# Taking all filler products off TensorE in a four-layer latent-attention kernel

## The reference, cut to what matters

```python
x = x + _L0_xattn_ref(_layernorm(x), ctx_1024, ctx_1024, fside, mask, ...)   # weighted, masked attention
x = x + _L0_attn_ref(_layernorm(x), ...)      # second-order Taylor attention
x = x + _L0_ffn_ref(_layernorm(x), ...)       # router and 8 experts, top 2
x = x + _L1_xattn_ref(_layernorm(x), ...)     # masked attention
x = x + _L1_attn_ref(_layernorm(x), ...)      # 16 heads of 64, block-causal
x = x + _L1_ffn_ref(_layernorm(x), ...)       # experts choose their tokens
x = x + _L2_xattn_ref(...)                    # key-masked attention
x = x + _L2_attn_ref(_layernorm(x), ...)      # plain attention
x = x + _L2_ffn_ref(_layernorm(x), ...)       # zone-weighted experts
x = x + _L3_xattn_ref(_layernorm(x), ...)
x = x + _L3_attn_ref(_layernorm(x), ...)      # gated recurrence over tokens
x = x + _L3_ffn_ref(_layernorm(x), ...)       # two-layer MLP
```

## Time and profile before

| | before |
|---|---|
| median of three executions | 1602.1 us (1601.02 to 1603.36) |
| the profiled execution, its own time | 1599.94 us |
| its span, first to last instruction | 1598.0 us |
| mean granted TensorE clock | 0.963 |
| PE busy | 1451.5 us (91%) |
| VectorE, ScalarE, GpSimd busy | 992.6, 713.4, 384.8 us |

### The profile page before, as it was taken

How to read it: one execution, slowest core, us unless ns; L and a number is a source line. 1 busy time by engine, 2 the same in 40 slices (tenths; PEclk the granted TensorE clock), 3 DMA queues, 4 the chain that set the end, 5 groups by cost and what they waited for, 6 DMA issues and landing times. The chain is left out here.

```text
span 1598.0 us, 29795 instructions
## 1 busy us (share of the span) xinstructions
PE 1451.5 (91%) x11197; PEld 845.2 (53%) x11296; DVE 992.6 (62%) x2290; ACT 713.4 (45%) x964; POOL 384.8 (24%) x548
## 2 busy tenths in 40 slices
PE   8899997999999988599999888499999896999987
PEld 3665653555555555255555464235555582555555
DVE  4544446888888744677777233298886235888842
ACT  4144130444444431166565442146767221667662
POOL 4543141666666620100000021111100001011000
PEclk9999997999999997799999999789999997999999
DMA  8888993434336043254552196146667611566700
GB/s 263 250 268 247 274 302 117 61 61 61 61 61 153 2 73 47 50 83 74 84 85 36 35 283 211 50 68 100 90 100 212 100 19 43 80 98 92 142 19 7
DMA packets 130377, 178.22 MB, mean 112 GB/s; under 512 B 14109, under 2 KB 105269, under 8 KB 123062
## 3 DMA queue, kind: packets, MB, share of 16 engines
q1 hardware_dynamic: 117802, 161.10, 47.7%
q10 hardware_dynamic: 12432, 15.21, 2.9%
HBM read 132.44 MB, written 43.78 MB: 110 GB/s over the span
## 5 line engine op out<-in xcount | busy, mean ns | idle before, releaser
L808 ACT ACTIVATE prob_a<-ps 128x1024 f32<-128x1024 f32 x512 | 505.2, 1023 | 304.3 <-PE ps L693 193.0
L676 PE MATMUL ps<-kop,qop 116*128 116x512 bf16 x1024 | 341.9, 404 | 57.1 <-PEq L529 33.3
L821 DVE CUSTOM_DVE_ANT_0 dump_a<-ps,neg_q 128x512 bf16<-128x512 f32 (+1 forms) x485 | 328.7, 717 | 98.5 <-PE ps L676 97.0
L690 PE MATMUL ps<-qop,kop 116*128 116x256 bf16 x2048 | 349.3, 274 | 10.2 <-ACT prob_a L808 4.9
L825 DVE TENSOR_REDUCE best_a<-ps 128x1 f32<-128x512 f32 (+1 forms) x488 | 312.6, 709 | 59.0 <-PE ps L676 58.9
L690 PEld LDWEIGHTS ps<-qop,kop 116*128 116x128 bf16 x2048 | 195.2, 100 | 137.3 <-ACT prob_a L808 18.0
L676 PEld LDWEIGHTS ps<-kop,qop 116*128 116x128 bf16 x1024 | 86.9, 100 | 216.8 <-issue 95.8
L715 PE MATMUL ps<-prob_a,vop_a 128*32 128x256 f32 x3072 | 185.0, 382 | 0.0
L920 POOL TENSOR_TENSOR used_a<-prob_a,gT 128x1024 f32<-128x1024 f32 x64 | 151.3, 2364 | 87.5 <-DVE used_a L838 67.4
L693 PE MATMUL ps<-neg_k,identb 128*128 128x512 bf16 x425 | 161.8, 381 | 0.0
L899 POOL CAST mpart_a<-nmax_a 128x2 bf16<-128x2 f32 x64 | 25.3, 396 | 560.1 <-DVE nmax_a L830 560.1
(11 more groups left out here) (309 smaller groups left out, 1296.4 us busy)
## 6 DMA issues: line engine op xcount, KB each, us to landing
kop<-kparts SPq DMA_DIRECT2D x448, 128.0 KB, 5.2
kparts<-kp SPq DMA_DIRECT2D x64, 384.0 KB, 4.5
vals<-vst SPq DMA_DIRECT2D x16, 1024.0 KB, 7.0
vraw<-vals SPq DMA_DIRECT2D x64, 256.0 KB, 6.4
e_w<-in_e_w SPq DMA_DIRECT2D x6, 2048.0 KB, 16.1
z_w<-in_z_w SPq DMA_DIRECT2D x24, 256.0 KB, 7.2
ctxT<-in_ctxT SPq DMA_DIRECT2D x8, 512.0 KB, 8.0
raw<-in_mask ACTq DMA_DIRECT2D x8, 512.0 KB, 5.9
```

The lines of the kernel that those rows point to most:

```text
L676: return pe.matmul(out, qop[0:R_ALL, h, t * P:(t + 1) * P], kop[0:R_ALL, h % UNROLL, j * CHUNK:(j + 1) * CHUNK], start=True, stop=True)
L690: ins = pe.matmul(st_bank(n)[:, j * NT:(j + 1) * NT], kop[0:R_ALL, h % UNROLL, k * P:(k + 1) * P], qop[0:R_ALL, h, :], start=(j % 2 == 0), ...
L808: act.activation(prob[:, n % NP, :], st_bank(n), ACT.Exp).then_inc(S("exp_done"), 1)
L821: dve.tensor_tensor_reduce(out=dump[:, k % 2, 0:width], in0=bank, in1=c.neg_q[:, t, j * CHUNK:j * CHUNK + width], scale=1.0, scalar=-3.0e3 ...
```

## The change

All calls of `keep_warm` and the function itself go, with the five constants that size them. No other instruction is added, moved or removed by the diff. Although the change's description says that the idle tile is no longer set, the diff does not touch line 507, where `c.idle` is set with four other tiles, nor the tile's declaration in line 2288.

```diff
@@ -39,8 +39,6 @@
-NORM_FILL, FOLD_FILL, TOP_FILL = 16, 6, 28
-SOFTMAX_FILL, SCAN_FILL = 12, 12
@@ -143,13 +141,6 @@
-def keep_warm(c, pe, n, bank=7):
-
-
-    for _ in range(n):
-        pe.matmul(c.ps[:, bank, :], c.identb[:, :], c.idle[:, :], start=True, stop=True)
@@ -783,7 +773,6 @@
             phase(range(NGROUP * H - W, NGROUP * H))
             fold(H - 1)
-            keep_warm(c, pe, FOLD_FILL, 3)
@@ -1042,7 +1031,6 @@
         @block.tensor
         def _(pe):
-            keep_warm(c, pe, NORM_FILL)
             pe.wait_ge(S("norm_done"), QT)
             turn_pe(c, pe, S, c.xn, 0, "turned")
...
@@ -1728,7 +1713,6 @@
             ins.then_inc(S("scores"), 1)
-            keep_warm(c, pe, TOP_FILL, 6)
@@ -1925,7 +1908,6 @@
             ins.then_inc(S("s_psum"), 1)
-            keep_warm(c, pe, SOFTMAX_FILL)
             pe.wait_ge(S("p_scaled"), QT)
@@ -2157,7 +2137,6 @@
-            keep_warm(c, pe, SCAN_FILL)
             pe.wait_ge(S("scanned"), CT)
```

## The result

| | before | after |
|---|---|---|
| median | 1601.56 us (1598.51 to 1603.36, 4 runs) | 1628.83 us (1627.56 to 1632.17, 4 runs) |
| profiled execution, span | 1598.0 us | 1626.5 us (own time 1628.41) |
| mean granted clock | 0.963 | 0.925 |
| predicted | | 1626 us (1611 to 1637) |

The ratio is 1.0175, 95% interval 1.0153 to 1.0198: the kernel became 27.3 us slower.

A forecast was written before the change was run, and what follows sets the result against it. The prediction took PE, busy 91% of the span, and single-file tails behind four attentions as the bound; 31.0 us lost to the clock, less 1.2 and 5.8, gave +24.0, so 1626 us, range 1611 to 1637.

The forecast's parts named there:

- Fillers in the way: Behind layer norms, attentions' ends, experts' choice and scan, products wait for fillers though their data are there: 5.8 us saved.
- part 1: The prediction's queue time saved: layer norms 1.5, attentions' ends 2.4, experts' choice 1.05, scan 0.88, in all 5.8 us.
- The clock falls at every layer norm: Eleven layer norms: the clock falls at each; nine groups of transposes lose 0.45 us each, 4.1 in all.
- The output projections: `project_out`, four times eight records at the attentions' ends: 1.3 us lost each, 5.2 in all.
- The sign that I had named: Profile after: the output projections would take 3.7 us in at least two of four.
- A long run loses 2.0: Long runs of products behind layer norms in six blocks lose 2.0 us each at the lower clock, 12.0 in all.
- the two groups of eight: `plain_attention` behind the softmax: two groups of eight records, at the lower level three times in four, 2.7 us lost.
- the bill: The prediction's list, block by block, of what the clock's falls cost without fillers: 31.0 us.
- The cover of 1.2 us: Inner parts of `taylor` and `frames`: VectorE or ScalarE end the wait, so 1.2 us is taken off the loss.
- Dear falls are fewer: Rival, 15%: each of eleven falls costs only 1.67 us and groups of eight escape; +12.6, 1615 us.
- Faster: Rival, 6%: the clock outlives the stands at the layer norms, only the queue time saved is left; -5.8, 1596 us.
- The lower level stays: Rival, 12%: in the thinly filled 42 us of `frames` the level isn't regained; +14 to +28 on top, some 1646 us.

The follow-up runs named there:

- e1: The kernel before with all 252 filler products kept at 512 columns but multiplying one row instead of 128: 1664.35 us, ratio 1.0374.
- e4: The kernel before with the number of fillers at each place sized to the length of its wait: 1595.78 us, ratio 0.9958.
- e8: The kernel before without the 48 fillers of the three queries blocks, all others kept: 1608.34 us, ratio 1.0045.
- e3: The kernel before without the 76 fillers at the attentions' ends, experts' choice, softmax and scan; layer norms keep theirs: 1615.79 us, ratio 1.0086.
- e6: The kernel before with half of every filler count, all places kept: 1611.93 us, ratio 1.0075.

## Why the prediction was right

It forecast +24 us (31.0 lost, less 1.2 and 5.8) by one mechanism, and the change measured +27.3. The mechanism is shown, by the granted clock and the same products' length in the rows and by e1. That the total came within 3 us is partly luck, as told below. (A small slip in the range: 3 us beyond 1615 and 1633 are 1612 and 1636, and the text has 1611 and 1637.)

**Fillers in the way: right.** The products follow their data by 0.05 us now: 580.20 to 580.25, and at the experts' choice 999.66 to 999.71. At the attentions' ends the way from `fold` to the first transpose fell from 574.98 - 572.78 = 2.20 to 570.81 - 569.46 = 1.35: 0.85 gained, where I had 0.6. e4 frees just these waits and gained about what part 1 has for them in the ends of the attentions, `plain_attention`, `recurrence` and the last block.

**The clock falls at every layer norm: right.** All transposes of `xn` behind a layer norm take 1.11 or 1.12, nine of nine; line 567 3.78 three times. Queries 1 and 3 cost 2.26 each, forecast 2.25.

**The output projections: right by their sum.** 3.78, 3.54, 3.10 and 3.55 instead of 1.99: on average 1.5 lost, forecast 1.3; with the gain of 0.85 that gives +0.7 a block, as forecast. Both terms were a little low and cancel. The sign that I had named, 3.7 in at least two of four, did not come: only one reached it.

**A long run loses 2.0: right by the sum, with a wide spread.** The first 16 records of `taylor` lost 1.40 (5.12; they take 3.72 at the higher level), `first_expert` 2.72, `frames` 1.65, `plain_attention` 2.50, `recurrence` 1.78 (5.50 against 3.72) and `feed_forward` 1.81: 11.9 together, forecast 12.0. What was short stands around these runs. Rows of `first_expert` and `plain_attention` before:

```profile
621.84 1.06 PE L161 MATMUL ps<-f_router,xT 128*128 128x8 f32 x8 [0.69 <-ACT xT L975]
622.75 7.15 PE L161 MATMUL ps<-f_w,xT 128*128 128x256 f32 x32
1257.77 3.72 PE L989 MATMUL ps<-xT,s_w 128*128 128x256 f32 x16 [0.69 <-ACT xT L975]
```

And of `first_expert`, `plain_attention` and `zone_experts` after:

```profile
622.08 1.87 PE L152 MATMUL ps<-f_router,xT 128*128 128x8 f32 x8 [0.69 <-ACT xT L964]
623.81 9.87 PE L152 MATMUL ps<-f_w,xT 128*128 128x256 f32 x32
1272.75 6.22 PE L978 MATMUL ps<-xT,s_w 128*128 128x256 f32 x16 [0.69 <-ACT xT L964]
1285.11 1.12 PE L141 MATMUL ps<-ident,s_p 128*128 128x128 f32 x4 [2.69 <-DVE s_p L1961]
1286.91 3.78 PE L1917 MATMUL ps<-s_pT,s_v 128*128 128x256 f32 x8 [0.69 <-ACT s_pT L1937]
1291.38 3.72 PE L152 MATMUL ps<-s_w,s_oT 128*128 128x256 f32 x8 [0.69 <-ACT s_oT L1940]
1301.91 1.87 PE L152 MATMUL ps<-z_router,xT 128*128 128x8 f32 x8 [0.69 <-ACT xT L964]
1303.63 9.58 PE L978 MATMUL ps<-xT,z_w 128*128 128x256 f32 x32
```

The routers, whose 8-column products stand at the head of a run, take 1.87 instead of 1.06 in both places: 0.8 each that I had priced at nothing. So were the softmax's transposes (0.45) and the experts' small products and transposes around the gather (1.45 after against 0.84, 1.06 against 0.60). In `plain_attention` the two groups of eight lost 1.8 and 1.7, both in full where I had three in four. The step that was short is the bill's list of what runs at the lower level: it has the large groups and leaves out the small ones in front of and between them, 3.1 us in all. The groups of eight at three in four add 0.8.

**The cover of 1.2 us wasn't there.** I took it off for the inner parts of `taylor` and `frames`. `taylor` lost 1.5 in its head and 0.6 more inside, where the level fell 2.9 us behind the first product with `t_kT` and not 5.3 (at 595.2; before at 598.4). `frames` lost 1.65 on its first 48 records (12.25 against 10.60) and fell once more inside, some 1.6 more:

```profile
926.34 12.25 PE L978 MATMUL ps<-xT,m_w 128*128 128x256 f32 x48 [1.75 <-DMA m_w<-in_m_w]
957.63 1.55 PE L1405 MATMUL ps<-m_pT,m_v 128*64 128x256 f32 x8
961.38 0.87 PE L1405 MATMUL ps<-m_pT,m_v 128*64 128x256 f32 x8
```

The wait for `m_w` hid the transposes, as forecast. The inner fall is not surely of the change: e8 has it too (+1.49), with every filler of `frames` in place. A slip of mine went the other way: the experts' transposes are in the bill twice, 0.45 too much.

**Two sizes cancel, and that is luck.** The tails cost 31.2, 7 more than the forecast of the whole; `project_context`, which the change doesn't touch, was 3.4 shorter in the profiled execution. The mean clock came out at 0.925, forecast about 0.93.

**The rivals.** *Dear falls are fewer* (1.67 each, and groups of eight escape): out. Two of the six runs lost no more than 1.67 (1.40 and 1.65), the others 1.8 to 2.7, and none of the groups of eight in the bill escaped. *Faster*: out, and e3 shows that even the short gaps cost. *The lower level stays*: `frames` was at the lower level for 3.4 us (957.0 to 960.4) of its inner 42 only; out. The Trainium skill's under 1% of a typical kernel's span for the penalty of ramping up ("TensorE: Matmul & The Clock Gate", Part 1) does not hold here: 1.75% more time was measured, with the fillers' own queue time already gained back, and the clock fell 27 times against 12.

## What to carry to other kernels

Where engines wait for each other in single file, count what the matrix engine's clock does in each wait before judging idle-time products useless; here 252 that nothing reads were worth 27 us of 1600. A filler has a price of its own: it holds up what stands behind it, and twice as long at the lower level (0.43 us against 0.22), so size each block to its wait (e4 gave another 5.5 us), with full-array products (the thin ones of e1 cost 63 us), and don't halve them (e6 lost 12.7). Judge such changes block by block, since one profiled execution's whole time hides a misplaced 3 us.

## What the runs showed of the hardware that was not expected

- Products of one row and 512 columns, as many as the full ones, left the clock at 0.917 where the full ones held 0.963, and took 0.43 us of the queue each at the lower level. In one place the level fell while they kept TensorE busy without a gap (587.4 to 590.2 us of e1).
- Removing two sets of fillers apart cost 25.1 and 14.5 us, together 27.3; 16 fillers that start at the lower level took up to 5.5 us of the queue instead of 3.6.
- With identical instructions, `project_context`'s length varied by 9 us between profiled executions (-3.4 to +5.3 against before). Before and after differ by 3.4 us in it with the clock low for the same 6.8 us.
